# Expert blocks of a routed feed-forward layer: gate and up products two steps ahead over three PSUM banks, a copy-out ring of eight, twelve shared blocks first

## The chip, the core and the metric

The kernel runs on one core of a Trainium2 chip. TensorE (PE) multiplies into eight PSUM banks; VectorE (DVE), ScalarE (ACT) and GpSimd (POOL) work on SBUF, the first two on PSUM too; SyncE (SP) only issues transfers here. Each engine takes its own instructions in the order in which they stand in the program, and engines wait for each other through semaphores. The metric is the time of one launch in microseconds (us), lower is better.

## The reference, cut to what matters

Four residual layers follow each other on 1024 rows of 256 values: windowed attention, a feed-forward layer with experts, full causal attention, and the same feed-forward layer once more. The change touches only the feed-forward layer, which runs twice:

```python
scores = softmax(x @ gate_w.T)                  # 16 experts
topk_w, topk_idx = top_k(scores, 4)             # 4 experts for a row
y = sum over experts e: cw[:, e] * ((silu(x @ wg[e].T) * (x @ wu[e].T)) @ wd[e].T)
y + (silu(x @ sw_gate.T) * (x @ sw_up.T)) @ sw_down.T    # shared expert, two slices of 176
```

## The kernel before, in words

**Blocks.** Each feed-forward stage is a list of 63 blocks of 128 rows. Sixteen are *shared* (8 row tiles times 2 slices of the shared expert, `("s", n)`) and 47 are *routed* (`("r", b)`): 128 slots of one expert, filled with rows that chose it. `ORDER` lists them: `FRONT` = 10 shared blocks, then pairs of routed and shared blocks in turn (two routed, two shared) until the shared ones are used up, and the rest routed. Below, m is a block's place in `ORDER`, and r15, say, the routed block number 15; from r6 on a routed block r*b* stands at place 16 + b.

**What a block takes.** For a routed block POOL gathers its rows from HBM (`gather`, L1045) into a ring of eight (`xg`, which is `z`). PE transposes them into bank 3 (`turn_x`, L1691), ACT and DVE split them into two float32r parts (`x_hi`, L1288; `x_lo`, L776). PE multiplies by gate and up weights (`gate_up`, six matmuls, L1466 through the helper `mm`), after reading the expert's offset into a register (`value_load`). ACT takes the silu (L1293), DVE multiplies it with the up half into `hb` (`mul`, L786 and L787), PE transposes the product (`turn_h`, L1719), ACT and DVE split it (`h_hi`, L1300; `h_lo`, L793), PE multiplies by the down weights (`down`, five matmuls). ACT copies the result into the ring `yb` of `YB_RING` = 4 (`y_out`, L1309), and POOL scatters it to HBM (`scatter`, L1054). A shared block needs no gather, transpose or scatter; DVE adds its result to `x` (L800).

**Order on the engines.** PE's step j issues `turn_x` for block j + 2 (if routed), `gate_up(j + 1)`, `turn_h(j)`, `down(j - 1)`. The steps of ACT and DVE follow the same pattern: ACT `x_hi` of block j + 2, `silu(j + 1)`, `h_hi(j)`, `y_out` of block j - 1; DVE `x_lo` of block j + 2, `mul(j + 1)`, `h_lo(j)`. In some steps a weight is split as well: ACT takes the high part (`expert_hi`, L1265, in the steps of `ACT_HI`), DVE the low part (`w_lo`, L769 and L770, in the steps of `DVE_LO`), and SP loads the weight after next when that is done. `gate_up` uses banks 0 and 1 in turn, `turn_h` bank 2 alone, `down` two more. `turn_x` waits for `x_lo` of the routed block before it.

**Routing.** The choice of experts (`normalized`, `picked`, `starts`, `places`, `hot`, `tables`) lies on DVE between steps 0 and 7, with small products on PE; the first gather waits for the table `sidx` that it ends with.

**POOL's order.** Eight gathers, then for each b `gather(b + 8)` and `scatter(b - 4)`. A gather waits until its ring slot has been transposed, a scatter until its block is copied out, and `y_out(b)` waits until `scatter(b - 4)` has landed.

**Tail.** SP waits for all scatters and reads the rows back (`gather_back`, `yg`, four transfers of 1 MB), and DVE adds them with their weights to `x` (L859). In the first stage SP has loaded the next layer's rotation table `rope` before that; POOL waits for it ahead of the next layer's `rstd` (L984), from which DVE makes `z` (L489).

Of the kernel before, what the change touches and what calls it, by code (L numbers as in the profile page):

```python
# [15 lines left out]
P = 128  # L16
# [36 lines left out]
NM = NSH + NB  # L53
FRONT = 10
ORDER = [("s", n) for n in range(FRONT)]
# [6 lines left out]
XG_RING = 8  # L62
YB_RING = 4
TILE_ROWS = TOPK * P + TOPK
# [16 lines left out]
def build(nc, d, out):  # L81
    ctx = ExitStack()
    with ctx:
# [19 lines left out]
        with own:  # L103
# [212 lines left out]
        def _(sp):  # L316
# [142 lines left out]
        def _(dve):  # L459
# [235 lines left out]
            def ffn(s, before):  # L695
# [84 lines left out]
                def mul(m):  # L780

                    dve.wait_ge(sem(f"{s}_silu"), since(s, "silu") + m + 1)
                    if m >= 2:
                        dve.wait_ge(sem(f"{s}_ht"), since(s, "ht") + m - 1)
                    u = m % 2
                    v.tensor_tensor(hb[:, u, 0:I_E], ps[:, u, I_E:GU], sg[:, u, :], ALU.mult)  # L786
                    v.tensor_tensor(hb[:, u, P + 64:P + 64 + I_E - P], ps[:, u, I_E + P:GU], sg[:, u, P:I_E],  # L787
                                    ALU.mult).then_inc(sem(f"{s}_h"), 1)

                def h_lo(m):  # L790

# [60 lines left out]
                for t0 in range(0, NT, 2):  # L852
                    for k in range(TOPK):
                        for t in (t0, t0 + 1):
                            if k == 0:
                                dve.wait_ge(sem(f"{s}_yl{t0 // 2}"), since(s, f"yl{t0 // 2}") + 16)
                            else:
# [118 lines left out]
        def _(pool):  # L976
# [49 lines left out]
            def ffn(s):  # L1026
# [48 lines left out]
                for b in range(NB - 4, NB):  # L1075
                    scatter(b)
# [66 lines left out]
        def _(act):  # L1143
# [137 lines left out]
            def ffn(s, before):  # L1281
# [8 lines left out]
                def silu(m):  # L1290

                    act.wait_ge(sem(f"{s}_gu"), since(s, "gu") + m + 1)
                    s_.activation(sg[:, m % 2, :], ps[:, m % 2, 0:I_E], ACT.Silu).then_inc(sem(f"{s}_silu"), 1)  # L1293

                def h_hi(m):

                    act.wait_ge(sem(f"{s}_ht"), since(s, "ht") + m + 1)
                    if m >= 2:
                        act.wait_ge(sem(f"{s}_down"), since(s, "down") + m - 1)
                    s_.copy(ht_hi[:, m % 2, :, :].rearrange("p c t -> p (c t)"), ps[:, 2, 0:2 * P]).then_inc(  # L1300
                        sem(f"{s}_h_hi"), 1)
# [160 lines left out]
        def _(pe):  # L1462
# [178 lines left out]
            def ffn(s, before):  # L1641
# [52 lines left out]
                def gate_up(m):  # L1694
# [6 lines left out]
                    else:  # L1701
# [8 lines left out]
                    three(ps[:, m % 2, 0:GU], rows,  # L1710
                          lambda c, b: operand(m, LO_AT * b + GU * c, GU)).then_inc(sem(f"{s}_gu"), 1)

                def turn_h(m):

                    pe.wait_ge(sem(f"{s}_h"), since(s, "h") + m + 1)
                    if m >= 1:
                        pe.wait_ge(sem(f"{s}_h_lo"), since(s, "h_lo") + m)
                    for c in range(2):
                        last = t_.transpose(ps[:, 2, P * c:P * c + P], hb[:, m % 2, P * c:P * c + P], idf[:, :])  # L1719
                    last.then_inc(sem(f"{s}_ht"), 1)  # L1720
# [23 lines left out]

                gate_up(0)
                for j in range(NM):
                    if j == 2:
# [5 lines left out]
                    elif j == 7:  # L1753
                        table(0)
                        table(1)
                    if j + 2 < NM and ORDER[j + 2][0] == "r":
                        turn_x(ORDER[j + 2][1])
                    if j + 1 < NM:
                        gate_up(j + 1)
                    turn_h(j)  # L1760
# [233 lines left out]

V_SPLIT_AT, W_LO_AT = 3, 6

OT_ALL = {"a": 2 * HA, "b": 2 * QPG * NG}
# [5 lines left out]
ACT_HI = {0: (2,), 1: (3,), 2: (4,), 3: (5,)}  # L2003
ACT_HI.update({6 + 2 * (n - POOL_LO): (n,) for n in range(POOL_LO, N_W)})
DVE_LO = {7 + 2 * (n - POOL_LO): (n,) for n in range(POOL_LO, N_W)}

# [4 lines left out]
def uses(u, ring):  # L2011

    return len(range(u, NB, ring))

F_TOTAL = {"ln": 2 * NT, "var": 2, "rstd": 2, "z": NT, "zt": 4, "xt_hi": 4, "xt_lo": 4,
           "consts": 32, "kc": 32, "wg_hi": 1, "wg_lo": 1, "logits": 2, "chosen": 2, "rank": 2, "hot": 2,
           "idx": 4, "route": 34, "ex": 1, "raw0": 16 * N_W // 2, "raw1": 16 * N_W // 2,
           "w_hi": N_W, "w_lo": 2 * POOL_LO, "w_lod": N_W - POOL_LO, "zs": 32, "gu": NM, "silu": NM, "h": NM, "ht": NM,
# [93 lines left out]
```

## Time and profile before

| | us |
|---|---|
| three runs | 1479.24, 1484.31 (median), 1486.74 |
| the profiled execution, its own time | 1483.01 |
| its span in the trace | 1481.2 |
| granted TensorE clock, mean over the span | 0.953 of full |
| PE busy, share of the span | 1309.8, 88% |
| DVE busy | 1042.3, 70% |
| ACT busy | 852.7, 58% |
| POOL busy | 851.5, 57% |
| silu of the first feed-forward stage, first and last | 391.8 to 564.7 |
| silu of both stages, first and last | 391.8 to 1453.4 |

The shares are averages over four different layers. The change can only act in the two feed-forward stages, some 180 us each, so those stages have to be read by themselves; the rows further down are from there. Times in rows count from the start of the span.

### The profile page before, as it was taken

How to read it: one execution, taken by the hardware profiler on the slowest of the kernel's cores; microseconds unless marked ns; L12 is line 12 of the kernel's file. 1: busy time of each engine (PE TensorE's matmuls, PEld its weight loads, DVE VectorE, ACT ScalarE, POOL GpSimd, SP SyncE). 2: the span in 40 equal slices, each digit the busy share in tenths (PEclk: the TensorE clock that was granted, in tenths of full speed). 3: DMA queues.
4: the chain of work that ended last, by engine and by line, in shares of the span. 5: the costliest groups of instructions: out<-in, count | busy, mean ns of one | idle time of the engine just before them, and what ended most of it. 6: DMA issues, size and time to landing. Idle time of an engine off the chain costs nothing.

```text
span 1481.2 us, 28548 instructions
## 1 busy us (share of the span) xinstructions
PE 1309.8 (88%) x8106; PEld 1098.7 (74%) x8106; DVE 1042.3 (70%) x2544; ACT 852.7 (58%) x2102; POOL 851.5 (57%) x752
## 2 busy tenths in 40 slices
PE   5999999999978986659999999899999998978893
PEld 3888888888877874547777777677777778877882
DVE  5676666646677546348888888788888887677545
ACT  1444444464436543248787878677878875436552
POOL 3555555530345772357787877677778650445772
PEclk9999999999979998869999999899999999979996
DMA  3000000002336335221222222122222202335334
GB/s 117 26 26 27 27 26 25 16 13 69 120 106 189 113 105 208 50 50 44 65 55 65 55 66 57 37 52 70 52 65 51 58 1 78 123 115 196 96 105 171
DMA packets 52271, 110.72 MB, mean 75 GB/s; under 512 B 11616, under 2 KB 21408, under 8 KB 51872
## 3 DMA queue, kind: packets, MB, share of 16 engines
q1 hardware_dynamic: 40992, 82.22, 19.3%
q0 software_dynamic: 9024, 24.65, 5.6%
q10 hardware_dynamic: 2112, 2.10, 0.4%
q8 instruction: 70, 1.15, 0.3%
q14 instruction: 73, 0.60, 0.1%
HBM read 64.11 MB, written 15.47 MB: 54 GB/s over the span
## 4 chain that ended last, share of the span: by engine, by line
PE 42%; issue 20%; POOL 17%; DVE 12%; DMA 4%; ACT 3%; POOLq 0%; SPq 0%; DVEq 0%; ACTq 0%
PE ps L1466 28%; PE ps L1621 7%; POOL pb_odd L1106 4%; POOL yt L1106 3%; PE ps L1831 2%; POOL z L1106 2%; POOL rb L1091 2%; DVE rb L548 2%; DVE x_res L859 2%; DMA raw_w<-in_wx 2%; POOL pb_low L1106 2%; POOL ra L1095 2%; PE ps L1691 1%; PE ps L1719 1%; PE ps L1553 1%
## 5 line engine op out<-in xcount | busy, mean ns | idle before, releaser
L918 DVE TENSOR_TENSOR pt_lo<-ps,pt_hi 128x512 fp32r<-128x512 f32 (+3 forms) x384 | 205.5, 548 | 53.3 <-ACT pt_hi L1385 47.7
L1466 PE MATMUL ps<-kh,qh 128*128 128x512 f32 (+3 forms) x768 | 204.4, 376 | 20.8 <-DMA qh<-qt_hi 9.0
L1385 ACT CAST pt_hi<-ps 128x512 fp32r<-128x512 f32 (+3 forms) x384 | 178.8, 481 | 59.8 <-PE ps L1831 51.7
L903 DVE TENSOR_REDUCE nmb<-ps 128x1 f32<-128x1024 f32 (+7 forms) x256 | 191.7, 749 | 28.3 <-PE ps L1466 27.2
L1466 PEld LDWEIGHTS ps<-kh,qh 128*128 128x128 f32 x768 | 132.2, 196 | 44.1 <-issue 12.9
L1466 PE MATMUL ps<-pt_hi,vst 128*128 128x512 f32 (+3 forms) x384 | 156.5, 408 | 1.8 <-DVE ra L883 1.8
L1045 POOL DMA_INDIRECT z<-zbuf,gidx x94 | 97.2, 1034 | 83.0 <-DVE sidx L763 30.3
L1466 PE MATMUL ps<-pt_lo,vst 128*128 128x512 f32 (+3 forms) x384 | 132.7, 349 | 0.0
L1183 ACT ACTIVATE pa<-sma,nmax 128x192 f32<-128x192 f32 x128 | 57.3, 449 | 129.4 <-DVE nmax L585 105.2
L1010 POOL TENSOR_TENSOR pa<-pa,rinv 128x384 f32<-128x384 f32 x64 | 53.0, 828 | 130.6 <-DVE rinv L593 130.6
L1054 POOL DMA_INDIRECT ybuf<-yb,sidx x94 | 95.1, 1012 | 40.8 <-issue 24.5
L1466 PE MATMUL ps<-w_ex,gx_hi 128*128 x376 | 101.7, 353 | 18.1 <-issue 12.0
L1106 POOL TENSOR_TENSOR pb_odd<-pb_odd,rib 128x1024 f32<-128x1024 f32 (+1 forms) x64 | 105.3, 1672 | 20.5 <-DVE rib L910 19.9
L1293 ACT ACTIVATE sg<-ps 128x176 f32<-128x176 f32 x126 | 40.1, 318 | 119.2 <-PE ps L1466 118.8
L1091 POOL TENSOR_TENSOR rb<-rb,rope 128x512 f32<-128x512 f32 x48 | 65.0, 1355 | 64.6 <-DMA rb<-raw 64.6
L1106 POOL TENSOR_TENSOR pb_low<-pb_low,rib 128x128 f32<-128x128 f32 (+2 forms) x96 | 58.2, 614 | 71.9 <-DVE rib L910 71.7
L548 DVE TENSOR_TENSOR rb<-ps,rope 64x512 f32<-64x512 f32 x128 | 88.1, 688 | 1.7
L1466 PEld LDWEIGHTS ps<-w_ex,gx_hi 128*128 128x128 f32 x376 | 63.6, 191 | 34.0 <-issue 31.2
L786 DVE TENSOR_TENSOR hb<-ps,sg 128x176 f32<-128x176 f32 x126 | 42.7, 339 | 65.3 <-ACT sg L1293 64.6
L984 POOL TENSOR_TENSOR rstd<-var,negh 128x4 f32<-128x4 f32 (+1 forms) x8 | 10.4, 1297 | 126.3 <-DVE var L477 120.3
L1106 POOL TENSOR_TENSOR yt<-yt,rib 128x768 f32<-128x768 f32 (+1 forms) x64 | 78.5, 1237 | 4.1 <-DVE rib L910 3.9
L1466 PEld LDWEIGHTS ps<-pt_hi,vst 128*128 128x128 f32 x384 | 75.0, 195 | 6.3 <-DVE ra L883 2.2
(225 smaller groups left out, 4162.6 us busy)
## 6 DMA issues: line engine op xcount, KB each, us to landing
raw_w<-in_wx SPq DMA_DIRECT2D x36, 608.0 KB
rb<-raw SPq DMA_DIRECT2D x192, 64.0 KB, 2.0
yg<-ybuf SPq DMA_DIRECT2D x8, 1024.0 KB, 8.0
qh<-qt_hi SPq DMA_DIRECT2D x64, 128.0 KB, 2.3
qh<-qt_lo SPq DMA_DIRECT2D x64, 128.0 KB, 2.4
wa<-in_wa SPq DMA_DIRECT2D x16, 384.0 KB, 3.0
wb<-in_wb SPq DMA_DIRECT2D x8, 384.0 KB, 3.4
wo_a<-in_wo_a SPq DMA_DIRECT2D x16, 128.0 KB, 2.0
```

What stands on the lines that cost most here:

```text
L548: last = v.tensor_tensor(rb[dst:dst + n, r, :], ps[src:src + n, bank, :], rope[src:src + n, 1, at], ALU.mult)
L903: v.tensor_reduce(nmb[:, par, i:i + 1], ps[:, b:b + 2, :].rearrange("p b k -> p (b k)")[:, 0:P * (t + 1)], AX.X, ALU.max, negate=True).the ...
L918: v.tensor_tensor(pt_lo[:, s % 3, at], ps[:, 4 + s % 2, at], pt_hi[:, s % 3, at].bitcast(F32), ALU.subtract).then_inc(sem("b_pt_lo"), 1)
L1010: g_.tensor_tensor(pa[:, two, 0:KW], pa[:, two, 0:KW], rinv[:, two].unsqueeze(2).broadcast_to([P, 2, KW]), ALU.mult).then_inc(sem("a_pn"), 1)
L1045: g_.indirect_dma_start(out=xg[:, u, :], out_offset=None, in_=zbuf[:, :], in_offset=bass.IndirectOffsetOnAxis(ap=gidx[:, b:b + 1], axis=0) ...
L1054: g_.indirect_dma_start(out=ybuf[:, :], out_offset=bass.IndirectOffsetOnAxis(ap=sidx[:, b:b + 1], axis=0), in_=yb[:, u, :], in_offset=None ...
L1091: g_.tensor_tensor(rb[:, r, :], rb[:, r, :], rope[:, 1, HALF * half:HALF * half + HALF], ALU.mult).then_inc(sem("b_sin"), 1)
L1106: g_.tensor_tensor(pb(par, t), pb(par, t), rib[:, par, i:i + 1].broadcast_to([P, P * (t + 1)]), ALU.mult).then_inc(sem("b_pn"), 1)
L1183: last = s_.activation(pa[:, t, 0:KW], sma[:, t, :], ACT.Exp, bias=nmax[:, t:t + 1], scale=-1.0, accum_out=rsum[:, t:t + 1])
L1385: s_.copy(pt_hi[:, s % 3, at], ps[:, 4 + s % 2, at]).then_inc(sem("b_pt_hi"), 1)
L1466: return t_.matmul(o, l, r, start=start, stop=stop)
L1621: ins = t_.matmul(o, (ot_hi, ot_lo)[a][s][:, n % OT_RING, P * m:P * m + P], wos[s][:, h, w, :], start=h == 0 and k == 0 and m % 2 == 0, st ...
```

## The change

`FRONT` becomes 12. `gate_up`, `silu` and `mul` run two steps ahead of `turn_h` instead of one, and `turn_x`, `x_hi` and `x_lo` three. From place 6 on (`DEEP`) `gate_up` goes round three banks and `turn_h` round two; the two added banks held the attention's second output half. The rings `hb` and `sg` stay at two. `YB_RING` becomes 8, and POOL scatters block b - 2 after gather b + 8 instead of block b - 4. The splits of the expert weights come one step earlier from the second expert on that DVE splits. The rotation table is loaded after the four transfers of `gather_back`. Memory for the larger ring comes from an unused hole and from `btri`, which now lies in the ring's last slot. Semaphores are reused, which adds no work.

```diff
-FRONT = 10
+FRONT = 12
-YB_RING = 4
+YB_RING = 8
+SCATTER_LAG = 2
...
+DEEP = 6
+def gate_bank(before, m):
+    return m % 2 if m < DEEP else (0, 1, ACC[before][1])[m % 3]
+def turned_bank(before, m):
+    return 2 if m < DEEP else (2, ACC[before][1] + 1)[m % 2]
...
 # SP
-            sp.wait_ge(sem("f_gu"), NM)
-            sp.dma_start(rope[:, :, :], d["rope_b"]).then_inc(sem("b_consts"), 16)
             sp.wait_ge(sem("f_down"), NM)
             sp.dma_start(maskb[:, :], d["maskb"]).then_inc(sem("b_consts"), 16)
             gather_back("f")
+            sp.dma_start(rope[:, :, :], d["rope_b"]).then_inc(sem("b_consts"), 16)
 # DVE, step(j); ACT the same with x_hi and silu
-                    if j + 2 < NM and ORDER[j + 2][0] == "r":
-                        x_lo(ORDER[j + 2][1])
-                    if j + 1 < NM:
-                        mul(j + 1)
+                    if j + 3 < NM and ORDER[j + 3][0] == "r":
+                        x_lo(ORDER[j + 3][1])
+                    if j + 2 < NM:
+                        mul(j + 2)
                     h_lo(j)
...
                 mul(0)
+                mul(1)
                 step(0)
                 normalized(s, 1)
 # POOL
-                    if b >= 4:
-                        scatter(b - 4)
+                    if b >= SCATTER_LAG:
+                        scatter(b - SCATTER_LAG)
 # PE, gate_up(m) and turn_h(m)
-                    if m >= 2:
+                    if m == DEEP + 2:
+                        pe.wait_ge(sem(f"{s}_xt_lo"), since(s, "xt_lo") + 4)
+                    if m >= DEEP + 2:
+                        pe.wait_ge(sem(f"{s}_h"), since(s, "h") + m - 2)
+                    elif m >= 2:
                         pe.wait_ge(sem(f"{s}_h"), since(s, "h") + m - 1)
...
-                    if m >= 1:
+                    if m > DEEP:
+                        pe.wait_ge(sem(f"{s}_h_lo"), since(s, "h_lo") + m - 1)
+                    elif m >= 1:
                         pe.wait_ge(sem(f"{s}_h_lo"), since(s, "h_lo") + m)
...
-                    if j + 2 < NM and ORDER[j + 2][0] == "r":
-                        turn_x(ORDER[j + 2][1])
-                    if j + 1 < NM:
-                        gate_up(j + 1)
+                    if j + 3 < NM and ORDER[j + 3][0] == "r":
+                        turn_x(ORDER[j + 3][1])
+                    if j + 2 < NM:
+                        gate_up(j + 2)
                     turn_h(j)
                     if j >= 1:
                         down(j - 1)
```

On POOL, this is where the first scatter stands in the first stage, before: `z<-zbuf` is a gather, `ybuf<-yb` a scatter.

```order
L1045 DMA z<-zbuf,gidx 128x256 x13
L1054 DMA ybuf<-yb,sidx 10272x256
L1045 DMA z<-zbuf,gidx 128x256
L1054 DMA ybuf<-yb,sidx 10272x256
L1045 DMA z<-zbuf,gidx 128x256
```

And after:

```order
L1045 DMA z<-zbuf,gidx 128x256 x11
L1054 DMA ybuf<-yb,sidx 10272x256
L1045 DMA z<-zbuf,gidx 128x256
L1054 DMA ybuf<-yb,sidx 10272x256
L1045 DMA z<-zbuf,gidx 128x256
```

Each scatter now stands two gathers further forward; their number and their turn-taking are the same.

On DVE, behind the first variance of the first stage, before (`hb<-ps,sg` twice is one `mul`, `z` the normalized second half, from which the routing of that half goes on):

```order
L786 TENSOR_TENSOR hb<-ps,sg 128x176
L787 TENSOR_TENSOR hb<-ps,sg 128x48
L786 TENSOR_TENSOR hb<-ps,sg 128x176
L787 TENSOR_TENSOR hb<-ps,sg 128x48
L793 TENSOR_TENSOR ht_lo<-ps,ht_hi 128x256
L489 TENSOR_SCALAR z<-x_res,mv,rstd 128x256 x4
```

And after:

```order
L785 TENSOR_TENSOR hb<-ps,sg 128x176
L786 TENSOR_TENSOR hb<-ps,sg 128x48
L785 TENSOR_TENSOR hb<-ps,sg 128x176
L786 TENSOR_TENSOR hb<-ps,sg 128x48
L785 TENSOR_TENSOR hb<-ps,sg 128x176
L786 TENSOR_TENSOR hb<-ps,sg 128x48
L792 TENSOR_TENSOR ht_lo<-ps,ht_hi 128x256
L488 TENSOR_SCALAR z<-x_res,mv,rstd 128x256 x4
```

A third `mul` has come in ahead of `z`.

On PE, around the transpose of the first gathered block (`ps<-idf,z`) in the first stage, before:

```order
L1691 MATMUL ps<-idf,z 128x128 x2
L1466 MATMUL ps<-w_sh,xt_hi 128x352 x2
L1466 MATMUL ps<-w_sh,xt_lo 128x352
L1466 MATMUL ps<-w_sh,xt_hi 128x352 x2
L1466 MATMUL ps<-w_sh,xt_lo 128x352
L1719 MATMUL ps<-idf,hb 128x128 x2
L1466 MATMUL ps<-w_sh,ht_hi 128x256 x2
```

And after, from the shared block whose products now stand ahead of it:

```order
L1467 MATMUL ps<-w_sh,xt_hi 128x352 x2
L1467 MATMUL ps<-w_sh,xt_lo 128x352
L1726 MATMUL ps<-idf,hb 128x128 x2
L1467 MATMUL ps<-w_sh,ht_hi 128x256 x2
L1467 MATMUL ps<-w_sh,ht_lo 128x256
L1467 MATMUL ps<-w_sh,ht_hi 128x256
L1467 MATMUL ps<-w_sh,ht_lo 128x256
L1692 MATMUL ps<-idf,z 128x128 x2
L1467 MATMUL ps<-w_sh,xt_hi 128x352 x2
```

The first transpose stands in PE's step 9 instead of 8, with eleven `gate_up` ahead of it instead of nine.

## Rows read from the trace of the kernel before

**Rows 1.** Busy time by stretch of the first stage, core 0, with granted clock

```profile
core 0: us, PE busy (x) PEld busy (x) DVE busy (x) ACT busy (x) POOL busy (x), PEclk, DMA share, GB/s
428.00:434.00 6.00, 4.22 (x18) 3.79 (x17) 3.60 (x13) 1.06 (x3) 4.55 (x4) 0.50 0.35 87
...
492.00:530.00 38.00, 37.95 (x263) 34.83 (x262) 20.95 (x70) 21.63 (x70) 28.24 (x29) 1.00 0.33 101
```

**Rows 2.** PE in order of time, front part; in brackets idle before and releaser

```profile
399.65 0.41 PE L1719 MATMUL ps<-idf,hb 128*128 128x128 f32 x2 [0.97 <-DVE ht_lo L793]
...
431.58 0.69 PE L1691 MATMUL ps<-idf,z 128*128 128x128 f32 x2 [1.78 <-DMA z<-zbuf,gidx]
...
435.62 0.59 PE L1466 MATMUL ps<-w_ex,gx_hi 128*128 x2 [0.36 <-issue]
...
1318.34 0.69 PE L1691 MATMUL ps<-idf,z 128*128 128x128 f32 x2 [1.60 <-DMA z<-zbuf,gidx]
```

**Rows 3.** One weight split on DVE, and PE's idle times beside such splits

```profile
482.61 1.15 DVE L769 TENSOR_TENSOR w_ex<-raw_w,w_ex 128x960 fp32r<-128x960 f32 x1
...
485.78 0.58 PE L1466 MATMUL ps<-w_ex,gx_hi 128*128 x2 [0.57 <-issue]
...
490.71 0.58 PE L1466 MATMUL ps<-w_ex,gx_hi 128*128 x2 [2.67 <-DVE gx_lo L776]
```

**Rows 4.** POOL in order of time: gathers (L1045) and scatters (L1054)

```profile
480.72 0.97 POOL L1045 DMA_INDIRECT z<-zbuf,gidx  x1 [0.30 <-issue]
...
486.20 0.97 POOL L1045 DMA_INDIRECT z<-zbuf,gidx  x1 [0.30 <-issue]
...
493.23 0.97 POOL L1045 DMA_INDIRECT z<-zbuf,gidx  x1 [1.85 <-ACT yb L1309]
...
547.18 0.97 POOL L1045 DMA_INDIRECT z<-zbuf,gidx  x1 [0.30 <-issue]
...
569.56 0.97 POOL L1054 DMA_INDIRECT ybuf<-yb,sidx  x1 [0.30 <-issue]
...
1458.22 0.97 POOL L1054 DMA_INDIRECT ybuf<-yb,sidx  x1 [0.30 <-issue]
```

**Rows 5.** ACT's copies of r13 (both stages) and r46, PE's transpose of r46

```profile
492.77 0.37 ACT L1309 COPY yb<-ps 128x256 f32<-128x256 f32 x1 [0.21 <-PE ps L1466]
...
561.05 0.38 PE L1691 MATMUL ps<-idf,z 128*128 128x128 f32 x2
...
568.35 0.37 ACT L1309 COPY yb<-ps 128x256 f32<-128x256 f32 x1 [0.81 <-PE ps L1466]
...
1380.67 0.37 ACT L1309 COPY yb<-ps 128x256 f32<-128x256 f32 x1 [0.69 <-PE ps L1466]
```

**Rows 6.** Waits from 492 to 570: who for whom, total, times, longest

```profile
ACT yb L1309 <- DMA ybuf<-yb,sidx: 8.0, 7, 2.6
```

**Rows 7.** The silus from 494 to 530, and landing times of all gathers

```profile
L1293 ACT ACTIVATE sg<-ps x17: 317/318/318, 494.2 to 529.3; 128x176 f32<-128x176 f32 x17
...
DMA to landing us min/median/max: 2.7/3.4/5.6
```

**Rows 8.** Front of the first stage: DVE's z, ACT's weight cast and what follows

```profile
395.51 0.72 DVE L489 TENSOR_SCALAR z<-x_res,mv,rstd 128x256 f32<-128x256 f32 x2
...
397.26 1.21 ACT L1265 CAST w_ex<-raw_w 128x1216 fp32r<-128x1216 f32 x1 [2.12 <-DMA raw_w<-in_wx]
...
398.84 0.60 ACT L1155 CAST xt_hi<-ps 128x512 fp32r<-128x512 f32 x1
```

**Rows 9.** Tail of the first stage; last row: KB and us from issue to landing

```profile
574.25 0.41 SPq L403 DMA_DIRECT2D wb<-in_wb  x1
...
585.34 1.15 POOL L984 TENSOR_TENSOR rstd<-var,negh 128x4 f32<-128x4 f32 x1 [12.95 <-DVE var L477]
...
588.27 1.06 DVE L489 TENSOR_SCALAR z<-x_res,mv,rstd 128x256 f32<-128x256 f32 x3
...
wb<-in_wb SPq DMA_DIRECT2D x1, 384.0 KB, 11.3
```

More of the change, by code:

```diff
@@ L855, in ffn @@
                             if k == 0:
-                                dve.wait_ge(sem(f"{s}_yl{t0 // 2}"), since(s, f"yl{t0 // 2}") + 16)
+                                dve.wait_ge(sem(f"{s}_{BACK[t0 // 2]}"), F_TOTAL[BACK[t0 // 2]] * (1 + (s == "g")))
                             else:
@@ L1072, in ffn @@
                         gather(b + XG_RING)
-                    if b >= 4:
-                        scatter(b - 4)
-                for b in range(NB - 4, NB):
+                    if b >= SCATTER_LAG:
+                        scatter(b - SCATTER_LAG)
+                for b in range(NB - SCATTER_LAG, NB):
                     scatter(b)
@@ L1292, in silu @@
                     act.wait_ge(sem(f"{s}_gu"), since(s, "gu") + m + 1)
-                    s_.activation(sg[:, m % 2, :], ps[:, m % 2, 0:I_E], ACT.Silu).then_inc(sem(f"{s}_silu"), 1)
+                    s_.activation(sg[:, m % 2, :], ps[:, gate_bank(before, m), 0:I_E], ACT.Silu).then_inc(sem(f"{s}_silu"), 1)
                 def h_hi(m):
@@ L1299, in h_hi @@
                         act.wait_ge(sem(f"{s}_down"), since(s, "down") + m - 1)
-                    s_.copy(ht_hi[:, m % 2, :, :].rearrange("p c t -> p (c t)"), ps[:, 2, 0:2 * P]).then_inc(
+                    s_.copy(ht_hi[:, m % 2, :, :].rearrange("p c t -> p (c t)"), ps[:, turned_bank(before, m), 0:2 * P]).then_inc(
                         sem(f"{s}_h_hi"), 1)
@@ L1311, in ffn @@
                 silu(0)
+                silu(1)
                 for j in range(NM):
-                    if j + 2 < NM and ORDER[j + 2][0] == "r":
-                        x_hi(ORDER[j + 2][1])
-                    if j + 1 < NM:
-                        silu(j + 1)
+                    if j + 3 < NM and ORDER[j + 3][0] == "r":
+                        x_hi(ORDER[j + 3][1])
+                    if j + 2 < NM:
+                        silu(j + 2)
                     h_hi(j)
@@ L1707, in gate_up @@
                         rows = lambda c, a: (gx_hi, gx_lo)[a][:, b % 2, c, :]
-                    if m >= 2:
+                    if m == DEEP + 2:
[3 more added lines that the diff above has]
+                    elif m >= 2:
                         pe.wait_ge(sem(f"{s}_h"), since(s, "h") + m - 1)
-                    three(ps[:, m % 2, 0:GU], rows,
+                    three(ps[:, gate_bank(before, m), 0:GU], rows,
                           lambda c, b: operand(m, LO_AT * b + GU * c, GU)).then_inc(sem(f"{s}_gu"), 1)
@@ L1715, in turn_h @@
                     pe.wait_ge(sem(f"{s}_h"), since(s, "h") + m + 1)
-                    if m >= 1:
+                    if m > DEEP:
+                        pe.wait_ge(sem(f"{s}_h_lo"), since(s, "h_lo") + m - 1)
+                    elif m >= 1:
                         pe.wait_ge(sem(f"{s}_h_lo"), since(s, "h_lo") + m)
                     for c in range(2):
-                        last = t_.transpose(ps[:, 2, P * c:P * c + P], hb[:, m % 2, P * c:P * c + P], idf[:, :])
+                        last = t_.transpose(ps[:, turned_bank(before, m), P * c:P * c + P], hb[:, m % 2, P * c:P * c + P], idf[:, :])
                     last.then_inc(sem(f"{s}_ht"), 1)
@@ L1745, in ffn @@
                 gate_up(0)
+                gate_up(1)
                 for j in range(NM):
@@ L2003 @@
 ACT_HI = {0: (2,), 1: (3,), 2: (4,), 3: (5,)}
-ACT_HI.update({6 + 2 * (n - POOL_LO): (n,) for n in range(POOL_LO, N_W)})
-DVE_LO = {7 + 2 * (n - POOL_LO): (n,) for n in range(POOL_LO, N_W)}
+ACT_HI.update({5 + 2 * (n - POOL_LO): (n,) for n in range(POOL_LO, N_W)})
+DVE_LO = {7: (POOL_LO,)}
+DVE_LO.update({6 + 2 * (n - POOL_LO): (n,) for n in range(POOL_LO + 1, N_W)})
 FIRST_PIECES = (0, 2, 1, 3, 4, 5)
```

21 lines of the change are left out of this document (10 added, 11 removed).

## The prediction

> **What bounds the kernel now.** I began with the page: four layers, PE busy 88% of the span. The change acts only in the two feed-forward stages, so the next view was the busy time by stretch. In the first stage PE is busy without a gap from 492 to 530, 37.95 of 38 us at full clock [rows 1]. There the silus, one for each block, come every (529.3 - 494.2)/16 = 2.19 us [rows 7]. No edit that only moves work makes that stretch shorter for PE. What can be won is PE's idle time before and behind it.
>
> PE in order of time shows it ahead of the stretch: 0.97 us at 399.65; 1.78 us at 431.58, where it waits for the first gather; 0.36 us at 435.62 [rows 2]; then, in each pair of steps with a weight split on DVE (1.15 us and a smaller part), some 0.57 us or more, and once 2.67 us, for the last expert's weights [rows 3].
>
> Behind the stretch the view of the waits names the copy-out: from 492 to 570 ACT's `y_out` waits 8.0 us in 7 places for scatters to land [rows 6]. Why are the scatters late? POOL in order of time answers: from 493.23, the gather of r25, to 547.18, that of r46, it makes 21 pairs of gather and scatter in 53.95 us, 2.57 us a pair, each transfer right behind the other (0.97 us and 0.30 us of issue) [rows 4]. PE takes 2.19 us a block. So POOL falls 0.38 us behind with each block, and a ring of four, with scatters four blocks back, passes that on to PE at about 530. POOL is the second bound of this stage, and it is the one that the ring hides or shows.
>
> **The ring and the lag.** The ring of eight takes away `y_out`'s wait: `scatter(b - 8)` is long landed. But POOL still has 47 gathers and 47 scatters in a fixed order. With the new lag `scatter(13)` stands ahead of `gather(24)`, and cannot go before r13 is copied out. From there POOL has no gap. I count from that copy, which ends at 492.77 + 0.37 = 493.14 [rows 5]. From copy to scatter I take what the last block shows, 569.56 - (568.35 + 0.37) = 0.84 us [rows 4, 5]. So `scatter(13)` goes at 493.98, `scatter(36)`, the last in a pair, 23 x 2.57 = 59.1 us later at 553.1, and `scatter(46)` after ten more of 1.27 us at 565.8. Before it went at 569.56.
>
> PE must allow that. From the same copy, 28 steps of 2.19 us bring it to the transpose of r46 at about 554.1. But `gather(46)` is issued at 551.8 and lands 3.4 us later (the median) at 555.2 [rows 7], so PE waits 1.1 us for it. Before, 8.5 us lay between that transpose (561.05) and the last scatter; it now stands a step further ahead, about 1.8 us, and 0.57 us of register load is laid open, as beside each such wait: 566.1. The two ends agree; the later one gives a gain of 3.5 us. In the second stage the copy ends at 1381.04, `scatter(46)` follows at 1453.7 to 1454.0 instead of 1458.22, a gain of 4.3 us, of which I take 4.0, since PE leaves the stall at low clock there. **Term 1: -7.5 us.**
>
> **Two ahead, and twelve first.** The deeper pipeline looks as if it freed PE everywhere. Step by step it does not. `turn_x(j + 3)` waits for `x_lo` of block j + 2, which DVE's step j - 1 makes first, behind the weight split that ends step j - 2; before, it was the same distance with all numbers one lower, and the splits move one step too. `mul(j + 2)` waits for `silu(j + 2)` in the step itself, as `mul(j + 1)` did, and `h_lo` follows it. So I leave all idle times of the split steps [rows 3] as they are, the 2.67 us too, since that weight and its user both move by one. What gets slack is `turn_h`, for which PE hardly waits there.
>
> The idle times of the front are different. At 399.65 `turn_h` waits, and an additional `gate_up` stands ahead of it. The table ends the routing at the same time as before, but two more shared blocks stand ahead of the first gathered one, so the 1.78 us and the 0.36 us are filled: 3.1 us in all, and in the second stage about as much (1.60 us at the gather) [rows 2]. Against it: from then on PE has one more `gate_up` and `turn_x` issued at any step. By columns streamed (6 x 352 and 2 x 128 of 3904 in 2.19 us) that is 1.3 us, which are not lost but come back only at the end of the stage, where POOL paces. And one more shared step, 3648 columns or 2.05 us, falls into the part in which the clock is 1.2 GHz (0.50 from 428 to 434 [rows 1]), some 1.0 us dearer. So r13 is copied out 3.1 - 1.3 - 1.0 = 0.8 us earlier. **Term 2: -1.6 us** in both stages.
>
> **The third mul.** It stands ahead of `z` on DVE and waits for the third `gate_up`, so `z` starts some 1.1 us later than 395.51 [rows 8]. Queued behind it is the whole routing of the second half. I cost it at nothing, because ACT, which takes the transposes of that `z`, is held by a weight cast until 398.47 (it waited for its load) and starts on them at 398.84 [rows 8]; they will be there by about 398.6. Without that cover it is 1.1 us in each stage.
>
> **The rotation table.** It now lands behind 4 MB of `yg`, and POOL's `rstd` waits for it. The transfer behind the four landed at 574.25 + 11.3 = 585.6; before `wb` (0.38 MB) comes now the table of 1 MB. The 4.4 MB of `yg` and `wb` landed in the 11.3 us after the last issue, so 1 MB takes 2.6 us, `wb`'s own part was 1.0 us, and the table lands at about 587.2; `rstd` (1.15 us) ends at 588.4 against a need at 588.27 [rows 9]. I take 0.2 us, and 0.2 us for four more waits of SP. **Term 3: +0.4 us.**
>
> **Sum.** -7.5 - 1.6 + 0.4 = -8.7 us. The profiled execution took 1483.0 us, so 1474.3; it lies 1.3 us under the median of the three runs, for which the forecast is 1475.6. The runs spread by 7.5 us, 0.5%, which is also about what can be told from no change; the gain is only just above it.
>
> **A rule of the Trainium skill.** Beside weight splits POOL's pair is longer: 5.48 us for two pairs from 480.72 to 486.20, 2.74 a pair, against 2.57 without [rows 4]. The page "SBUF — State Buffer" (Terms) says that VectorE and GpSimd share one port pair, locked for a whole instruction. By the difference of those rows the rule costs 0.17 us a pair in split steps; beside DVE's other work the rows show none. If it held wherever DVE works, term 1 would be gone; that is rival 2.
>
> **Rivals.**
> 1. *As summed*, -8.7 us, from -5 to -12: chance 0.50. For it: the 53.95 us without a gap.
> 2. *POOL's pair stays at 2.74 us behind the splits.* DVE is closer behind PE, with more of its work beside POOL's. 23 x 0.17 = 3.9 us in each stage eats term 1; -0.9 us remain, 1483.4. Gathers landing nearer 5.6 us than 3.4, or the third `mul` uncovered, lead halfway there. Chance 0.27. Against it: 21 pairs at 2.57 with DVE half busy.
> 3. *TensorE's clock rises earlier.* It was at 1.2 GHz from 428 to 434, with the idle time of 1.78 us in that stretch [rows 1, 2]. With that filled it may rise sooner; at most that gives back half of PE's 4.2 busy us there, 2.1 us in each stage: -13. If the waits beside splits shrink as well, though I find no way, six times 0.57 us in each stage come to it: -20, 1465. Chance 0.17. The skill's page "TensorE: Matmul & The Clock Gate" (Part 1) has sustained activity release the clock, which points here.
> 4. *Slower: the shorter lag starves the gathers.* `gather(b + 8)` now stands behind a scatter that needs a fresh copy. If POOL's pair came to 2.95 us, the pairs cost 23 x 0.38 = 8.7 us more in each stage, 17.4 in all: +8.7 us, 1493. It decides from 2.76 us on, where the gain is zero. Chance 0.06.
>
> **Numbers.** The likeliest is rival 1, 1475.6, own range 1472 to 1479. For 8 in 10 I reach down into rival 3 and up through rival 2: 1466 to 1485. Faster by over 0.5% (7.4 us): 0.38 of rival 1 and all of rival 3, 0.55. Slower: 0.05. Between: 0.40.
>
> **What would show it.** Right, step by step: `y_out` waits for no scatter; POOL without a gap at 2.57 us a pair from the copy of r13, and the last gather waited for by PE; the idle time at the first gather gone; idle times beside splits as before, and the 2.67 us still there; `rstd` released by the rope load or just not. Wrong: PE idle at `turn_x` for gathers long before r40 (rival 4); pairs of 2.74 us behind 492 (rival 2); split steps of PE shorter than before (my reading of the deeper pipeline); or a first gather that PE waits for.

## The result and the profile after

| | before | after |
|---|---|---|
| median (range, runs), us | 1486.08 (1479.24 to 1489.75, 20) | 1479.32 (1475.97 to 1482.72, 20) |
| profiled execution: own time / span | 1483.01 / 1481.2 | 1478.16 / 1476.1 |
| first silu to start of last scatter, stage 1 / stage 2 | 177.80 / 179.54 | 176.37 / 174.71 |
| PE busy | 1309.8 | 1303.8 |

The ratio of after to before is 0.9961, 95% interval 0.9950 to 0.9972: 5.8 us faster. The forecast was 8.7 us, 1475.6, with 1466 to 1485 as its range; the change lands in "within 0.5%". Slow executions are left out of the ratios and medians, such as one of `l4_all` that took 1501.16 us at 0.824 of the full clock.

The third row of the table measures a feed-forward stage by itself, without the attention layers, whose clock differs from execution to execution (below). By it stage 2 gained 4.8 us, as forecast, and stage 1 gained 1.4 of the 4.3 us forecast. The agreement in stage 2 is partly chance: in the profiled execution of before the clock stayed low there from 1376 to 1383, behind the stall for the last expert, and in after from 1376 to 1379.

Busy time by stretch of after, first the front of stage 1 and then the stretch behind the last weight split (columns as in [rows 1]):

```profile
428.00:430.00 2.00, 2.00 (x11) 1.93 (x10) 1.90 (x10) 1.54 (x3) 1.18 (x1) 0.50 0.02 4
430.00:432.00 2.00, 2.00 (x15) 1.98 (x14) 1.71 (x6) 0.85 (x3) 1.67 (x2) 0.83 0.25 66
432.00:434.00 2.00, 2.00 (x16) 1.81 (x14) 1.99 (x5) 0.96 (x3) 1.70 (x2) 1.00 0.81 177
...
492.00:530.00 38.00, 37.57 (x259) 34.71 (x259) 20.78 (x69) 21.06 (x68) 29.00 (x30) 1.00 0.34 102
```

The same front in the kernel before:

```profile
430.00:432.00 2.00, 0.42 (x3) 0.42 (x3) 1.28 (x3) 0.00 (x0) 1.70 (x2) 0.50 0.19 66
432.00:434.00 2.00, 2.00 (x9) 1.93 (x8) 0.42 (x1) 0.38 (x1) 1.67 (x2) 0.50 0.83 192
434.00:436.00 2.00, 1.64 (x12) 1.41 (x11) 1.20 (x4) 1.83 (x4) 1.41 (x2) 0.92 0.81 324
```

Two things stand there: the wait for the first gather is gone (PE busy 2.00 instead of 0.42 at 430), and the granted clock is up at about 430.7 instead of 434.3, full speed of 2.4 GHz where before it was 1.2. The second is no accident of one execution: in all ten profiled kernels with twelve shared blocks first the clock is up between 429.1 and 432.0, in the four with ten first between 434.3 and 437.5 (busy time by stretches of 1 us).

PE of after in order of time, only rows with idle time ahead of them (these answer to [rows 2, 3]):

```profile
434.83 0.41 PE L1692 MATMUL ps<-idf,z 128*128 128x128 f32 x2 [0.79 <-DVE gx_lo L775]
436.02 0.59 PE L1467 MATMUL ps<-w_ex,gx_hi 128*128 x2 [0.78 <-issue]
...
454.06 0.41 PE L1692 MATMUL ps<-idf,z 128*128 128x128 f32 x2 [0.79 <-DVE gx_lo L775]
455.08 0.59 PE L1467 MATMUL ps<-w_ex,gx_hi 128*128 x2 [0.61 <-issue]
459.59 0.41 PE L1692 MATMUL ps<-idf,z 128*128 128x128 f32 x2 [0.37 <-DVE gx_lo L775]
...
465.40 0.41 PE L1692 MATMUL ps<-idf,z 128*128 128x128 f32 x2 [0.79 <-DVE gx_lo L775]
...
487.93 0.59 PE L1467 MATMUL ps<-w_ex,gx_hi 128*128 x2 [2.63 <-DVE gx_lo L775]
...
557.42 0.44 PE L1692 MATMUL ps<-idf,z 128*128 128x128 f32 x2 [0.35 <-DMA z<-zbuf,gidx]
558.38 0.59 PE L1467 MATMUL ps<-w_ex,gx_hi 128*128 x2 [0.52 <-issue]
```

The waits beside splits are longer than before, up to 0.79 + 0.61 us (one wait for DVE and one called "issue"). From 434 to 492 PE is busy 46.17 of 58 us; before it was 48.72 (both from the busy time by stretch). The stall for the last expert is the same 2.63 us, and the last gather is now waited for.

POOL of after in order of time (g22, s12, g23, s13; then g46; then three of the last scatters, s43, s44 and s46), which answers to [rows 4]:

```profile
487.66 0.97 POOL L1045 DMA_INDIRECT z<-zbuf,gidx  x1 [0.31 <-issue]
492.13 0.99 POOL L1054 DMA_INDIRECT ybuf<-yb,sidx  x1 [3.49 <-ACT yb L1309]
493.42 0.97 POOL L1045 DMA_INDIRECT z<-zbuf,gidx  x1 [0.30 <-issue]
494.73 0.99 POOL L1054 DMA_INDIRECT ybuf<-yb,sidx  x1 [0.34 <-issue]
...
552.53 0.97 POOL L1045 DMA_INDIRECT z<-zbuf,gidx  x1 [0.30 <-issue]
...
563.75 0.97 POOL L1054 DMA_INDIRECT ybuf<-yb,sidx  x1 [1.20 <-ACT yb L1309]
565.10 1.33 POOL L1054 DMA_INDIRECT ybuf<-yb,sidx  x1 [0.38 <-issue]
...
568.08 0.97 POOL L1054 DMA_INDIRECT ybuf<-yb,sidx  x1 [0.38 <-issue]
```

From g23 to g46 there are 23 pairs in 59.11 us, 2.57 us each, without a gap. In front of them stands a wait of 3.49 us: `scatter(12)` is behind the copy of r12, and that copy is behind the stall of 2.63 us. Who waits for whom from 492 to 570 (compare [rows 6]; the wait for scatters is gone):

```profile
POOL ybuf L1054 <- issue: 9.1, 29, 0.4
ACT yb L1309 <- PE ps L1467: 9.0, 33, 1.1
...
POOL ybuf L1054 <- ACT yb L1309: 5.9, 6, 3.5
...
PE ps L1692 <- DMA z<-zbuf,gidx: 0.3, 1, 0.3
```

The tail of stage 1 on POOL and DVE (compare [rows 9]):

```profile
585.77 1.36 POOL L984 TENSOR_TENSOR rstd<-var,negh 128x4 f32<-128x4 f32 x1 [14.85 <-DMA rope<-in_rope_b]
...
587.17 1.39 DVE L488 TENSOR_SCALAR z<-x_res,mv,rstd 128x256 f32<-128x256 f32 x4
```

`z` comes 1.10 us earlier than before (588.27), the last scatter 1.48 us (569.56 to 568.08): 0.38 us went in the tail.

### The profile page after: what moved, and what is told of

It reads as the page before. It is cut to its first block, busy times and chain, and to the rows that moved or that the text cites. A ratio compares the mean times of both kernels' runs of the same rounds, so it can differ in the third digit from the quotient of the medians.

```text
span 1476.1 us, 28546 instructions
## 1 busy us (share of the span) xinstructions
PE 1303.8 (88%) x8106; PEld 1096.7 (74%) x8106; DVE 1040.7 (71%) x2544; ACT 852.2 (58%) x2102; POOL 850.2 (58%) x752
## 4 chain that ended last, share of the span: by engine, by line
PE 42%; issue 20%; POOL 17%; DVE 13%; DMA 3%; ACT 3%; SPq 0%; POOLq 0%; DVEq 0%; ACTq 0%
PE ps L1467 28%; PE ps L1622 7%; POOL pb_odd L1106 4%; POOL yt L1106 3%; PE ps L1839 2%; POOL rb L1091 2%; POOL z L1106 2%; DVE rb L547 2%; POOL pb_low L1106 2%; POOL ra L1095 1%; PE ps L1692 1%; PE ps L1554 1%; DMA raw_w<-in_wx 1%; PE ps L1726 1%; DVE x_res L859 1%
## 5 line engine op out<-in xcount | busy, mean ns | idle before, releaser
L1045 POOL DMA_INDIRECT z<-zbuf,gidx x94 | 97.1, 1033 | 61.5 <-DVE sidx L762 30.2
L1054 POOL DMA_INDIRECT ybuf<-yb,sidx x94 | 93.9, 999 | 57.1 <-issue 28.9
L1091 POOL TENSOR_TENSOR rb<-rb,rope 128x512 f32<-128x512 f32 x48 | 64.8, 1350 | 64.6 <-DMA rb<-raw 64.6
```

What stands on the lines that cost most here:

```text
L1045: g_.indirect_dma_start(out=xg[:, u, :], out_offset=None, in_=zbuf[:, :], in_offset=bass.IndirectOffsetOnAxis(ap=gidx[:, b:b + 1], axis=0) ...
L1054: g_.indirect_dma_start(out=ybuf[:, :], out_offset=bass.IndirectOffsetOnAxis(ap=sidx[:, b:b + 1], axis=0), in_=yb[:, u, :], in_offset=None ...
L1091: g_.tensor_tensor(rb[:, r, :], rb[:, r, :], rope[:, 1, HALF * half:HALF * half + HALF], ALU.mult).then_inc(sem("b_sin"), 1)
```

## The experiments

The gains in us in the text are differences of ratios times the 1486.1 of before; each ratio is against executions of before from the same batch, so the medians of different rows compare less well. "Ahead" is by how many steps `gate_up` runs ahead of `turn_h`. "Stage 1 / 2" is again first silu to start of the last scatter, from the one profiled execution of each kernel; an asterisk marks a stage in which the clock fell behind the last expert's stall.

| kernel | ring | lag | ahead | FRONT | ratio (95%) | median | stage 1 / 2 |
|---|---|---|---|---|---|---|---|
| before | 4 | 4 | 1 | 10 | 1 | 1486.1 | 177.8 / 179.5* |
| after | 8 | 2 | 2 | 12 | 0.9961 (0.9950–0.9972) | 1479.3 | 176.4* / 174.7* |
| ring_alone | 8 | 2 | 1 | 10 | 0.9956 (0.9941–0.9972) | 1479.0 | 176.6* / 173.8 |
| old_ring | 4 | 4 | 2 | 12 | 0.9975 (0.9963–0.9987) | 1480.6 | 176.9* / 176.2* |
| front10 | 8 | 2 | 2 | 10 | 1.0045 (1.0028–1.0062) | 1491.4 | 180.3 / 179.8 |
| lag4 | 8 | 4 | 2 | 12 | 0.9921 (0.9904–0.9938) | 1473.1 | 171.1 / 171.3 |
| ring_lag4_alone | 8 | 4 | 1 | 10 | 0.9947 (0.9933–0.9962) | 1477.2 | 173.8 / 173.7 |
| one_ahead | 8 | 4 | 1 | 12 | 0.9924 (0.9896–0.9952) | 1474.1 | 173.1* / 172.2* |
| l4_last | 8 | 4 | 2 | 12 | 0.9881 (0.9865–0.9897) | 1468.1 | 172.4 / 170.0 |
| l4_offset | 8 | 4 | 2 | 12 | 0.9869 (0.9852–0.9885) | 1464.8 | 169.1 / 166.6* |
| l4_parity | 8 | 4 | 2 | 12 | 0.9904 (0.9888–0.9920) | 1470.9 | 172.3 / 172.4* |
| offset_lag2 | 8 | 2 | 2 | 12 | 0.9919 (0.9896–0.9942) | 1472.7 | 172.6 / 171.6 |
| both_lag4 | 8 | 4 | 2 | 12 | 0.9852 (0.9825–0.9879) | 1464.2 | 170.0 / 168.1 |
| l4_all | 8 | 4 | 2 | 12 | 0.9839 (0.9814–0.9865) | 1460.9 | 166.5 / 167.2 |

**The ring and the lag by themselves.** The kernel before with these edits. With a ring of eight the slots lie where the rotation table goes, so the table's load has to stand behind the scatters; term 3 comes with term 1 and was not measured apart.

```diff
-YB_RING = 4
+YB_RING = 8
+SCATTER_LAG = 2
```

> The kernel before with the ring of eight and the lag of two only (and the rotation table loaded behind the read-back, since the longer ring lies in its memory); FRONT 10, products one step ahead. Theory A (term 1 was sized rightly, POOL paces from the copy of r13, and the deeper pipeline costs at the split steps): scatter(46) of the first stage at 566.1, of the second at about 1450.5, -7.1 us on the time before, or no more than 1 us behind the full change. Rival B (term 1 was too large, and the deeper pipeline neither helps nor hurts): scatter(46) of the first stage near 568, -4 to -5 us.

Measured: -6.5 us, as fast as the full change. The size is A's, but the last scatter of stage 1 went at 568.56, where B had it; stage 2's went at 1452.82. In stage 1 POOL waited for copies twice about the stall (2.87 and 0.96 us), the second time behind a stretch in which PE ran at half clock, from 492 to 496.

**The rest by itself.** The changed kernel with ring and lag as before.

```diff
-YB_RING = 8
-SCATTER_LAG = 2
+YB_RING = 4
+SCATTER_LAG = 4
```

> The changed kernel with the ring of four, scatters four blocks back: what is left is two steps ahead, twelve first, splits a step earlier. As predicted (term 2 and 3): -1.2 us on the time before. Theory A: it is no faster than before, 0 to +2 us, since silu(31) comes 0.6 us later per stage, and copy-outs wait for scatters again. Rival B: -1 to 0 us.

Measured: -3.7 us, more than any of the expectations. With terms of -6.5 (ring, lag and table) and -3.7 the full change should have given some -10; it gave -5.8. So some 4 us are lost where the two meet. By the three intervals that is good to about ±3.4 us: the loss is shown, its size only roughly.

**Twelve first.**

```diff
-FRONT = 12
+FRONT = 10
```

> The changed kernel with FRONT = 10. As predicted: the first gather is waited for again; 3.1 - 1.0 us are lost in each stage against the changed kernel, +4.2 us, 1483.5. Theory A: +2 to +4, and idle times beside splits that have a shared addition in the same DVE step stay at 0.8 + 0.6 us, since places of shared additions (even steps) fall on split steps (even) with 10 as with 12. Rival: nothing is lost, since POOL paces the stage's end: within 1 us of the changed kernel.

Measured: +6.7 us against before, 12.5 us against after; every expectation was far too low. PE's first transpose of a gathered block, in order of time:

```profile
431.48 0.69 PE L1692 MATMUL ps<-idf,z 128*128 128x128 f32 x2 [5.00 <-DMA z<-zbuf,gidx]
```

and the stretch behind it:

```profile
432.00:434.00 2.00, 2.00 (x9) 1.93 (x9) 0.42 (x1) 0.41 (x2) 1.39 (x3) 0.50 0.33 70
434.00:436.00 2.00, 2.00 (x11) 2.00 (x10) 1.54 (x4) 1.88 (x4) 1.61 (x2) 0.50 0.48 139
436.00:438.00 2.00, 2.00 (x11) 1.93 (x10) 1.27 (x5) 0.61 (x3) 1.47 (x2) 0.61 0.35 92
```

A transpose three places ahead meets the first gather one step sooner. PE stands still for 5.00 us and then runs at half clock until 437. Twelve first is what pays for the deeper pipeline. (Of the 12.0 us between the profiled executions 3.9 are in stage 1 and 5.1 in stage 2. The other 2.9 lie between the last scatter of stage 1 and the first silu of stage 2; over all 14 profiles that stretch takes 708.9 to 714.1 us, so they are within its spread.)

**The lag back to four, the rest as changed.**

```diff
-SCATTER_LAG = 2
+SCATTER_LAG = 4
```

> The changed kernel with the scatters four blocks back again, ring still of eight. If the lag of two helps, as it takes scatters off the end: 1 to 3 us slower than the changed kernel. Theory A: with the lag of two POOL waits 3.5 us for the copy of r12 at 488.6; with four it has copied blocks to scatter meanwhile, so scatter(46) comes 1 to 2.5 us earlier in each stage, -2 to -5 us against the changed kernel, and the last gather is no longer waited for.

Measured: 1473.1, 11.7 us faster than before and 5.9 us faster than after, a little more than A expected. POOL of this kernel in stage 1 (g24, s12; then g46, s46):

```profile
487.66 0.97 POOL L1045 DMA_INDIRECT z<-zbuf,gidx  x1 [0.30 <-issue]
491.17 0.99 POOL L1054 DMA_INDIRECT ybuf<-yb,sidx  x1 [2.54 <-ACT yb L1309]
...
546.53 0.97 POOL L1045 DMA_INDIRECT z<-zbuf,gidx  x1 [0.30 <-issue]
...
563.67 0.97 POOL L1054 DMA_INDIRECT ybuf<-yb,sidx  x1 [0.38 <-issue]
```

The same `scatter(12)` waits for the same stall, but POOL has two more gathers behind it by then (g24 instead of g22). g46 goes at 546.53 instead of 552.53, and PE never waits for it. From the 33rd silu to the last PE takes 66.09 us in stage 1 and 66.03 in stage 2; in after it takes 69.04 and 68.03. That is 5 us of waits and opened register loads which the shorter lag laid on PE. The stages differ by 8.7 us in all; 2.2 of the rest are the clock, which fell behind the stall in both stages of after and in neither of lag4.

**The ring alone with the old lag.** The edit is that of ring_alone, but with `SCATTER_LAG = 4`.

> The kernel before with the ring of eight alone: scatters four blocks back as they were, products one step ahead, FRONT 10, the rotation table behind the read-back. Theory C (once POOL is not held by a short lag, PE paces the end, so what the ring saves and what the deeper pipeline saves add up): about 3 to 5 us slower than the kernel with all of the change and a lag of four (1473.1), 1476 to 1478. Rival D (the lag was the whole fault, and two ahead with twelve first is worth nothing): 1473, as fast as the kernel with everything and a lag of four. The lag's own cost, by either: this is 1 to 6 us faster than the ring with a lag of two alone (1479.0).

Measured: -7.9 us; C holds and D falls. Against ring_alone the lag makes no measurable difference here (0.9947 and 0.9956). With lag four the parts add up: 0.0053 + 0.0025 = 0.0078, and lag4 measured 0.0079. With lag two they do not: 0.0044 + 0.0025 = 0.0069, and after measured 0.0039. (Each part holds the moved table, so its +0.4 us is in both sums twice.)

**One step ahead, twelve first.** The kernel of ring_lag4_alone with `FRONT = 12`.

> Products one step ahead as in the kernel before, but FRONT = 12, ring of eight, lag of four: of the change only two steps ahead (with its banks and the earlier splits) is left out. Theory F (the 3.9 us between 0.9947 and 0.9921 come from the twelve shared blocks, which cover the first gather and let the clock rise sooner, and two ahead adds nothing): 1470 to 1474, ratio about 0.992 or below. Rival G (they need both; two ahead has a part of its own in hiding the waits for silu and product): 1475 to 1478, ratio 0.994 to 0.9955.

Measured: 0.9924, as fast as lag4 (0.9921); F is favoured. The interval is wide, ±0.0028, and that of lag4 is ±0.0017, so for two ahead a gain or a loss of up to some 5 us can't be excluded. Its profile has something on both sides. PE in order of time at the front of this kernel:

```profile
399.00 0.41 PE L1718 MATMUL ps<-idf,hb 128*128 128x128 f32 x2 [1.44 <-DVE ht_lo L792]
```

That wait is absent with two ahead (0.97 us in [rows 2]). But from 434 to 485, at full clock in both, PE is busy 43.68 us here and 41.98 in lag4. The clock is up at 429.6 here too, so its early rise comes with twelve first and not with two ahead.

**The last expert's weight a step earlier** (on lag4).

```diff
+ACT_HI[26] = ACT_HI.pop(27)
+DVE_LO[27] = DVE_LO.pop(28)
```

> All of the change with a lag of four, and the last expert's weight split one step earlier on ACT and DVE (steps 26 and 27 for 27 and 28). Theory C (PE paces the end): the idle time of 2.64 us at the last expert shrinks to the usual 0.3 + 0.57 us, -1.7 us in each stage, and no clock falls behind it, which cost 1.1 to 1.5 us where it happened: -3.4 to -5 us against 1473.1. Rival E (POOL paces it after all): the stall moves to a later wait for a gather, 0 to -1 us.

Measured: -5.9 us against lag4; C, a little above its upper end. The two profiled executions don't show it (lag4's is the fastest of its runs, 1469.8, and this one, 1471.0, the slowest of its own), so the size stands on the timed runs alone, and their intervals leave it at ±3.5 us. PE in order of time where the 2.63 us stood:

```profile
484.96 0.41 PE L1692 MATMUL ps<-idf,z 128*128 128x128 f32 x2 [0.63 <-DVE gx_lo L775]
485.97 0.58 PE L1467 MATMUL ps<-w_ex,gx_hi 128*128 x2 [0.60 <-issue]
488.58 0.59 PE L1467 MATMUL ps<-w_ex,gx_hi 128*128 x2 [0.35 <-issue]
```

**The offset read ahead of the transpose** (on lag4).

`read_offset` is the `value_load` taken out of `gate_up`.

```diff
+                    if j + 2 < NM:
+                        read_offset(j + 2)
                     if j + 3 < NM and ORDER[j + 3][0] == "r":
                         turn_x(ORDER[j + 3][1])
```

> All of the change with a lag of four, and PE reads a block's weight offset into its register ahead of the transpose in its step instead of behind it. Theory C: the idle times of 0.57 us ahead of gate_up, nine in each stage, are the time of that read, laid open each time PE waited before it; they go, the waits in front of the transposes stay, -4 to -5 us in each stage, less what other waits take over; -5 to -8 us in all. Rival: the 0.57 us are PE's restart after any wait; they stay, 0 us.

Measured: -7.7 us against lag4 (±3.5), as expected. All the rows with idle time on PE from 452 to 470:

```profile
454.11 0.41 PE L1692 MATMUL ps<-idf,z 128*128 128x128 f32 x2 [0.81 <-DVE gx_lo L775]
458.94 0.41 PE L1692 MATMUL ps<-idf,z 128*128 128x128 f32 x2 [0.24 <-DVE gx_lo L775]
464.18 0.41 PE L1692 MATMUL ps<-idf,z 128*128 128x128 f32 x2 [0.79 <-DVE gx_lo L775]
469.05 0.41 PE L1692 MATMUL ps<-idf,z 128*128 128x128 f32 x2 [0.38 <-DVE gx_lo L775]
```

The waits ahead of transposes are as in after; the 0.57 to 0.61 us "issue" ahead of `gate_up` are gone. They were the register load, and not a restart of PE behind any wait, since the waits are still there.

**No split beside a shared addition** (on lag4).

```diff
+DVE_LO = {step: (n,) for n, step in zip(range(POOL_LO, N_W), (7, 9, 11, 13, 15, 17, 19, 21, 22, 24, 26, 28))}
...
```

The omitted lines move ACT's high parts along.

> All of the change with a lag of four, and the weight splits of the seventh to thirteenth expert back in the odd steps, one step later, so that none shares a DVE step with a shared addition (steps 12, 16, 20); from the fourteenth on as they were. If the shared addition of 0.41 us in the same step is what makes the idle time 0.79 us at three of the transposes instead of 0.37: those three go to 0.4 or less, -1.2 us in each stage, -2.4 us against 1473.1. If not: no change, or slower where a weight comes late.

Measured: 0.9904 against 0.9921, 2.5 us, which is inside the two intervals; inconclusive. The waits of 0.79 us were gone in stage 1, but one of 1.06 us and two of 0.53 and 0.56 us for DVE came in their place, the register loads stayed, and the stages of its profiled execution were not shorter.

**The offset read early, with the lag of two.**

> The changed kernel with its lag of two, and the weight offsets read ahead of the transposes. With the lag of four that edit gave 0.0052, 7.7 us. If the lag of two lets POOL pace the second half of the stage, so that what PE gains in the split steps is lost on POOL, about half of it or less arrives here: 0.9935 to 0.996 against the time before. If the lag only costs a fixed 3 us a stage, all of it arrives: 0.991.

Measured: 0.9919, so 6.2 of the 7.7 us arrive; nearer to "all of it" than to "half". But it stands 7.4 us behind l4_offset, and its PE waits for gathers again, 4.5 us in seven waits from 492 to 570, the longest this one:

```profile
550.13 0.44 PE L1692 MATMUL ps<-idf,z 128*128 128x128 f32 x2 [2.10 <-DMA z<-zbuf,gidx]
```

The lag of two costs about as much here as in the changed kernel.

**Together.** Both edits on lag4, and then the odd splits as well.

> All of the change with a lag of four, the last expert's weight split one step earlier, and the weight offsets read ahead of the transposes. If PE paces the end of both stages, the two gains add up: 0.9921 - 0.0040 - 0.0052 = 0.983, 1460 us. If with the offsets read earlier the stall at the last expert is already part gone (it was 1.85 instead of 2.64 us in that run) or POOL becomes the bound: 0.985 or more, 1462 to 1464.

> The kernel of both_lag4 with the splits of the seventh to thirteenth expert in odd steps as well. The odd steps gave 0.0017 by themselves (0.9921 to 0.9904); if that adds up, 0.981 to 0.982, 1457 to 1458 us; if PE's waits for the first parts of blocks 22 to 24, which grew there (1.06 us at one transpose), eat it, as fast as both_lag4.

Measured: 0.9852 and 0.9839. Both beat before and after clearly. The sum of the two edits would be 0.983, just inside the interval of both_lag4, so whether they add up in full stays open; reading the offset early already cuts the stall to 1.85 us, which speaks against it. Between the two, and against l4_offset (0.9869), the intervals overlap.

## Why the prediction was right in its range and too large by 3 us

**Term 1, the ring, -7.5 us: right.** The copy-out waits are gone, POOL makes pairs of 2.57 us, the last gather is waited for, and ring_alone measures -6.5 us with the +0.4 of term 3 in it. By stages its profile does not split as I had it: 1.2 us in stage 1 and 5.7 in stage 2, against 3.5 and 4.0. The clock fell behind the stall in stage 1 of ring_alone and in stage 2 of before, which tilts the two that way. Rival 2 is out: 23 pairs kept 2.57 us while DVE worked. What was wrong in it is where the chain begins. I let it start at the copy of r13, 0.8 us earlier than before. But the stall of 2.63 us, ahead of `gate_up` of r15, now stands in PE's step ahead of `down` of r12, and the lag of two puts `scatter(12)` behind that copy. `scatter(13)` went at 494.73, not at 493.2, and the last scatter at 568.08 instead of 565.3: 1.5 us at the start, 0.9 us for a late copy at 563.75, the rest in small pieces.

**The step that failed is the sum.** I added term 2 to term 1. Measured alone they are -6.5 and -3.7 us (each with term 3), together -5.8. A transpose three places ahead wants each gather a block sooner, while the lag of two puts each gather behind a scatter that needs a fresher copy. So what PE gained in front was lost in waits for POOL. I had this only as rival 4, as a pair of 2.95 us; it came as some 2 to 3 us in each stage, with pairs of 2.57. The counter-test is lag4: 5.9 us faster than the changed kernel, while with one step ahead and ten first the same edit changes nothing measurable. Whether the depth or the twelve blocks in front make the lag of two dear is not separated: no kernel has one step ahead, twelve first and a lag of two.

**Term 2, -1.6 us: mechanism right in part, size wrong both ways.** The first gather's wait went as predicted. The clock rose 3.6 us sooner as well, which I had put under rival 3 and not into the term; "a shared step at low clock, +1.0" did not come. (Nor did its size follow from its own figures: a step of 2.05 us at full clock would take some 2 us more at half the clock.) Against it, "I leave all idle times of the split steps as they are" failed: from 434 to 492 PE was busy 2.55 us less than before, and already 3.15 us less by 485 (44.96 and 41.81), ahead of the stall and the low clock behind it. DVE of after shows one place:

```profile
451.54 0.41 DVE L799 TENSOR_TENSOR x_res<-x_res,ps 128x256 f32<-128x256 f32 x1
451.87 1.15 DVE L768 TENSOR_TENSOR w_ex<-raw_w,w_ex 128x960 fp32r<-128x960 f32 x1
453.04 0.42 DVE L769 TENSOR_TENSOR w_ex<-raw_w,w_ex 48x256 fp32r<-48x256 f32 x1
453.49 0.42 DVE L775 TENSOR_TENSOR gx_lo<-ps,gx_hi 128x256 fp32r<-128x256 f32 x1
```

The splits moved by one step and the shared blocks by two, so that the shared addition (L799) now stands directly ahead of a split. Where a transpose of a gathered block follows (432 to 465, four times), PE waits 0.79, 0.56, 0.79 and 0.79 us; behind the other splits it waits 0.24 to 0.40. Before had one such wait too, 0.86 us at 453.62, without an addition directly ahead of the split, so the rows point at the coincidence and don't prove it; and that it costs time in all was not shown, since l4_parity was inconclusive. The stall of the last expert stayed, as predicted.

My list of PE's idle times in front had left out the longest, in which PE waits for DVE behind the routing. The change did not touch it; before and after:

```profile
415.25 0.66 PE L1719 MATMUL ps<-idf,hb 128*128 128x128 f32 x2 [4.83 <-DVE ht_lo L793]
415.34 0.66 PE L1726 MATMUL ps<-idf,hb 128*128 128x128 f32 x2 [4.77 <-DVE ht_lo L792]
```

**Luck.** Term 2, measured with term 3 in old_ring, gave 3.7 us where the two were put at 1.2, and the loss where the two terms meet, some 4 us, was not in the sum at all. These errors have opposite signs, so that the total missed by only 3 us is in part luck.

**The third `mul`: right.** `z` starts at 396.64 instead of 395.51, 1.1 us later, and ACT takes its transposes at 398.95 instead of 398.84. **Term 3, +0.4 us: right**; the tail lost 0.38 us, with `rstd` released by the rotation table at 585.77.

**What neither term held.** Behind the stall PE's clock fell to 0.50 in both stages of after, and in stage 2 alone of before. The gap between silus next behind the stall is 3.28 us in stage 1 of after and 2.20 before: 1.1 of the 2.9 us by which stage 1 missed its forecast. And all that stage 1 had gained at `z` (1.1 us) was gone at the start of stage 2 (first silu 1278.60 and 1278.68), with a clock of 0.83 from 810 to 820 in an attention layer that the change does not touch, where before had 1.00. I take that for a difference of executions, not of kernels: the 20 runs of after spread by 7 us, those of before by 11, and each kernel has one profile.

## What to carry to other kernels

When a change deepens a pipeline and retunes a queue's order at once, ask of each queue which instruction its unbroken chain starts behind, and whether both edits move that point in the same direction; gains of a consumer and of a producer don't add where the one's slack was the other's. Test the lag apart from the ring: the ring gave the slots, and with the deeper pipeline the old lag used them better. An idle time called "issue" of one constant size behind every wait is worth a look: here it was a register load standing behind the wait instead of ahead of it, and moving it gave 7.7 us on top of lag4, where the whole change gave 5.8.

## What the chip showed that I had not expected

The clock behind a short stall was a matter of chance here. After about 2.6 us without work PE's granted clock fell in 9 of the 18 profiled stages of the nine kernels that have this stall, as here in after:

```profile
488.00:490.00 2.00, 2.00 (x10) 1.94 (x11) 0.02 (x1) 0.41 (x2) 0.63 (x1) 0.67 0.36 111
490.00:492.00 2.00, 2.00 (x10) 2.00 (x9) 0.96 (x4) 1.02 (x3) 0.00 (x0) 0.50 0.00 0
492.00:494.00 2.00, 2.00 (x16) 1.98 (x16) 1.02 (x4) 1.01 (x4) 1.57 (x2) 0.97 0.19 66
```

Of the ten stages of the five kernels in which the stall was 1.85 us or less it fell in one, stage 2 of l4_offset, right behind 1.85 us:

```profile
1360.00:1362.00 2.00, 0.20 (x2) 0.00 (x0) 1.96 (x5) 0.65 (x2) 1.70 (x2) 1.00 0.27 84
1362.00:1364.00 2.00, 1.95 (x10) 1.89 (x11) 0.31 (x1) 0.38 (x2) 1.39 (x3) 0.73 0.18 66
1364.00:1366.00 2.00, 2.00 (x10) 2.00 (x10) 0.95 (x4) 1.05 (x3) 1.70 (x2) 0.50 0.43 135
```

It also fell to 0.50 in three places away from that stall, each time behind two shorter waits with one transpose between them: in before at 1424 (1.28 and 0.57 us), in l4_last at 438 (0.85 and 0.77) and in l4_parity at 1350 (0.71 and 0.88). So a shorter stall does not make the clock safe; by these counts it falls less often. That would fit with l4_last's 5.9 us, where two stalls cut by 1.7 us each promised 3.4, but lag4's own profile shows no fall behind the stall, so it is argued, not shown. The Trainium skill's page "TensorE: Matmul & The Clock Gate" (Part 1) says that the same kernel meets slow matmuls at its start in differing number from run to run. No kernel here was profiled twice; the two stages of one kernel differ in that way here, as in before, where the stall of stage 1 left the clock at 1.00 and that of stage 2 did not.

PE's register load lays open 0.57 to 0.61 us between a transpose of 0.41 us and the next matmul when it stands behind a wait, and nothing that the rows show when it stands ahead of it (l4_offset).
